# The 71 expert tiles of a Mamba-and-experts block: TensorE's program as straight code, with the weight buffer's half as a register in the address

## What is computed

```python
x = layernorm(x + mamba_layers(x))                      # two layers, states scanned over 512 steps
logits = x @ gate_w + gate_b                            # 8 experts
weights, indices = top_k(logits, 2); weights = softmax(weights)
h = x @ w1[e] + b1[e]                                   # 256 -> 2048, for expert e
xh, gh = split(h, 2)
out_e = (silu(gh) * xh) @ w2[e] + b2[e]                 # 1024 -> 256
x = layernorm(x + sum over the two experts of weight * out_e)
```

## Time and profile before

| | us |
|---|---|
| median of three runs | 1474.63 (1473.24 to 1475.08) |
| the profiled execution | 1472.57 |
| its span, from the first to the last instruction | 1470.7 |
| PE busy with matmuls | 1297.4 (88%) |
| DVE busy | 1087.3 (74%) |
| POOL busy | 807.9 (55%) |
| ACT busy | 791.8 (54%) |

### The profile page before, as it was taken

The page is one execution under the profiler, slowest core; times in us unless marked ns, Lnnn a source line. Parts: engine busy times, 40 slices in busy tenths (PEclk is TensorE's granted clock), DMA queues, the critical chain, the costliest instruction groups (busy, mean ns, idle before and its releaser), DMA issues.

```text
span 1470.7 us, 40051 instructions
## 1 busy us (share of the span) xinstructions
PE 1297.4 (88%) x13108; PEld 1028.9 (70%) x13109; DVE 1087.3 (74%) x2499; ACT 791.8 (54%) x1814; POOL 807.9 (55%) x740
## 2 busy tenths in 40 slices
PE   3889999999999998999872899999999999999970
PEld 1456666656666666666651799999999999999970
DVE  5889999999998898888876566565666565565537
ACT  4656666666666576656540444445444444444434
POOL 2466776766675787677874246060346061052771
PEclk9999999999999998999975899999999999999985
DMA  5203443323343323322512431303030303102594
GB/s 185 98 29 116 130 129 108 97 91 118 103 130 116 108 85 112 115 76 83 180 40 97 148 116 32 118 29 116 31 118 29 121 29 114 36 29 64 136 203 146
DMA packets 94653, 145.70 MB, mean 99 GB/s; under 512 B 13488, under 2 KB 77488, under 8 KB 94448
## 3 DMA queue, kind: packets, MB, share of 16 engines
q1 hardware_dynamic: 79216, 97.06, 20.7%
q0 software_dynamic: 15072, 46.51, 10.6%
q10 hardware_dynamic: 288, 1.19, 0.2%
HBM read 103.06 MB, written 41.67 MB: 98 GB/s over the span
## 4 chain that ended last, share of the span: by engine, by line
PE 60%; DVE 15%; issue 10%; POOL 8%; ACT 3%; SPq 2%; DMA 2%; DVEq 0%; ACTq 0%; POOLq 0%
PE pe L998 13%; PE pa L998 13%; PE py L1010 12%; PE pa L620 4%; PE py L720 3%; POOL arena L2230 3%; DVE arena L1508 3%; PE pa L612 3%; PE pm L756 3%; PE pz L709 2%; PE pt L738 2%; DVE arena L1547 2%; DVE arena L1574 1%; DVE arena L1522 1%; POOL arena L2220 1%
## 5 line engine op out<-in xcount | busy, mean ns | idle before, releaser
L998 PE MATMUL pe<-arena 128*128 128x128 f16 x3408 | 218.5, 220 | 22.5 <-issue 22.5
L998 PEld LDWEIGHTS pe<-arena 128*128 128x128 f16 x3408 | 202.4, 98 | 28.2 <-issue 27.4
L998 PE MATMUL pa<-arena 128*128 128x128 f16 x3408 | 216.1, 219 | 0.0
L1404 ACT ACTIVATE arena<-pe,arena 128x128 f32<-128x128 f32 x568 | 162.2, 372 | 85.1 <-PE pe L998 84.9
L998 PEld LDWEIGHTS pa<-arena 128*128 128x128 f16 x3408 | 198.7, 97 | 0.0
L1010 PE MATMUL py<-arena 128*128 x1704 | 197.6, 273 | 0.8 <-DVE arena L2008 0.8
L1508 DVE SCALAR_TENSOR_TENSOR arena<-pa,arena 128x511 f32<-128x511 f32 (+2 forms) x240 | 178.6, 745 | 7.5 <-ACT arena L1073 1.1
L1980 DVE SCALAR_TENSOR_TENSOR pm<-pa,arena 128x128 f32<-128x128 f32 x284 | 80.6, 352 | 138.1 <-ACT arena L1404 122.6
L1010 PEld LDWEIGHTS py<-arena 128*128 128x128 f16 x1704 | 163.6, 98 | 18.8 <-issue 1.1
L720 PEld LDWEIGHTS py<-arena 128*128 128x128 f32 x1024 | 129.8, 204 | 35.4 <-issue 22.9
L2133 POOL TENSOR_SCALAR arena<-arena 128x1536 f16<-128x1536 f32 (+2 forms) x35 | 42.7, 1220 | 201.8 <-DVE arena L2008 196.8
(11 more groups left out here) (225 smaller groups left out, 2532.5 us busy)
## 6 DMA issues: line engine op xcount, KB each, us to landing
arena<-step_rows SPq DMA_DIRECT2D x64, 512.0 KB, 6.4
arena<-in_w_exp POOLq DMA_DIRECT2D x32, 768.0 KB
arena<-queue SPq DMA_DIRECT2D x74, 129.5 KB, 2.1
answer<-arena SPq DMA_DIRECT2D x71, 128.0 KB, 1.7
arena<-in_x SPq DMA_DIRECT2D x16, 512.0 KB, 6.6
answer<-zeros SPq DMA_DIRECT2D x10, 512.0 KB, 4.7
arena<-h SPq DMA_DIRECT2D x9, 512.0 KB, 6.2
h<-arena SPq DMA_DIRECT2D x8, 512.0 KB, 3.0
```

Source lines behind the costliest of these rows:

```text
L998: ins = pe.matmul(bank[:, f * P:(f + 1) * P], w_split[:, p, hl, d * 2 * FF + col:d * 2 * FF + col + P], x[:, r, d, :], start=(n == 0), sto ...
L1404: ins = e.activation(sg[:, half, f, :], GATE[half][:, f * P:(f + 1) * P], ACT.Silu, bias=b1a[:, bass.ds(ex_, 1), ff], scale=1.0 / S1)
```

## The change

PE's expert stage is written out tile by tile: no loop, no branch on the parity, constant thresholds, no cut through a hidden part. In `hidden` the weights' address is `part(p, ...)` with p as a register, as in `result`. `experts` loads one value per group as before, now ahead of the group's first tile, and the plan no longer holds the two parities. `part` itself, `turn` and `result` stay.

```diff
             def experts(i):
-                v = pe.value_load(plan_i[0:1, bass.ds(i + 2 * NJT, 1)], min_val=0, max_val=2047)
-                return [v % 8, (v // 8) % 8, (v // 64) % 8], (v // 512) % 2, v // 1024
+                v = pe.value_load(plan_i[0:1, bass.ds(i + 2 * NJT, 1)], min_val=0, max_val=511)
+                return [v % 8, (v // 8) % 8, v // 64]
...
-            def hidden(i, r, ex_, halves=(0, 1)):
+            def hidden(i, r, ex_):
                 turn(i, r + 1)
                 pe.wait_ge(w_have, ex_ + 1)
                 pe.sem_inc(hop, 1)
-                by_parity(i, r, ex_ % 2, halves)
-
-            def by_parity(i, r, odd, halves):
-                with pe.If(odd < 1):
-                    products(i, r, 0, halves)
-                with pe.Else():
-                    products(i, r, 1, halves)
-
-            def products(i, r, p, halves):
-                j = WB * i + r
-                for half in halves:
+                j, p = WB * i + r, ex_ % 2
+                for half in range(2):
...
-                                ins = pe.matmul(bank[:, f * P:(f + 1) * P], w_split[:, p, hl, d * 2 * FF + col:d * 2 * FF + col + P],
+                                ins = pe.matmul(bank[:, f * P:(f + 1) * P], part(p, hl, d * 2 * FF + col, P),
                                                 x[:, r, d, :], start=(n == 0), stop=(n == len(passes) - 1))
...
-            ex_, _, _ = experts(0)
-            hidden(0, 0, ex_[0])
-            hidden(0, 1, ex_[1])
-            result(0, 0, ex_[0] % 2)
-            hidden(0, 2, ex_[2], (0,))
-            def whole_group(i):
-                ex_, odd1, odd2 = experts(i)
-                by_parity(i - 1, 2, odd1, (1,))
-                result(i - 1, 1, odd2)
-                hidden(i, 0, ex_[0])
-                result(i - 1, 2, odd1)
-                hidden(i, 1, ex_[1])
-                result(i, 0, ex_[0] % 2)
-                hidden(i, 2, ex_[2], (0,))
-            with pe.Fori(1, NGRP) as i:
-                whole_group(i)
...
+            before = None
+            for i in range(NGRP + 1):
+                ex_ = experts(i)
+                for r in range(WB if i < NGRP else NLEFT):
+                    hidden(i, r, ex_[r])
+                    if before is not None:
+                        result(*before)
+                    before = (i, r, ex_[r] % 2)
+            result(*before)
...
-            dve.tensor_reduce(stj[0:1], cmp_nt[0:1], AX.X, ALU.add)
-            step(dve.tensor_tensor(cmp_[0:1], cmp_[0:1], sign[0:1, :].unsqueeze(1).to_broadcast([1, NJT, NE]), ALU.mult))
-            step(dve.tensor_reduce(ej[0:1], cmp_[0:1, :, 0:NE - 1], AX.X, ALU.add))
+            step(dve.tensor_reduce(stj[0:1], cmp_nt[0:1], AX.X, ALU.add))
...
-            for m in (1, 2):
-                step(dve.scalar_tensor_tensor(packed[:, 1:NG], odd[:, 0:NG - 1, WB - m], float(m * NE ** WB),
-                                              packed[:, 1:NG], ALU.mult, ALU.add))
...
-            pool.iota(sign_i[:, :], [[0, NE // 2], [-2, 2]], base=1, channel_multiplier=0)
...
-            pool.tensor_copy(sign[:, :], sign_i[:, :])
```

More of the change, by code:

```diff
@@ L190, in build @@
         jdum_i = sb("jdum_i", [P, NJT], I32)
-        sign_i = sb("sign_i", [P, NE], I32)
-        sign = sb("sign", [P, NE])
         ARENA = 50400
@@ L286, in build @@
         cmp_, cmp_nt = carve(NJT, NE), carve(NJT, NE)
-        ej, stj, usedj, tmpj = carve(NJT), carve(NJT), carve(NJT), carve(NJT)
+        stj, usedj, tmpj = carve(NJT), carve(NJT), carve(NJT)
         plan_f = carve(3 * NJT + 2 * NE + WB)
@@ L1897, in _ @@
             step(dve.tensor_tensor(cmp_nt[0:1], cmp_[0:1], nt[0:1].unsqueeze(1).to_broadcast([1, NJT, NE]), ALU.mult))
-            dve.tensor_reduce(stj[0:1], cmp_nt[0:1], AX.X, ALU.add)
-            step(dve.tensor_tensor(cmp_[0:1], cmp_[0:1], sign[0:1, :].unsqueeze(1).to_broadcast([1, NJT, NE]), ALU.mult))
-            step(dve.tensor_reduce(ej[0:1], cmp_[0:1, :, 0:NE - 1], AX.X, ALU.add))
+            step(dve.tensor_reduce(stj[0:1], cmp_nt[0:1], AX.X, ALU.add))
             NG = NJT // WB
-            number, odd = e_f.rearrange("p (g r) -> p g r", r=WB), ej[0:1].rearrange("p (g r) -> p g r", r=WB)
+            number = e_f.rearrange("p (g r) -> p g r", r=WB)
             packed = par_f[:, 0:NG]
```

## The result

The changed kernel takes 1667.0 us (median of 4, 1663.48 to 1671.85) against 1474.9 us beside it: a ratio of 1.131 (95% interval 1.129 to 1.133), so 13% slower. The forecast was 1635 us with a range of 1595 to 1700. The profiled execution took 1666.63 us, its span is 1664.9 us.

The account below looks back on a forecast made before the run. The bound was to move from PE to its sequencer: first hidden matmul at 812.2 us, 71 tiles of 10.95 us, 1.4 and 2 us at the end, 35.6 closing, run overhead: 1632.7, rounded up to 1635 us, range 1595 to 1700.

Parts of the forecast that it names:

- the main case: Expert stage bound by PE's sequencer at full clock, 0.127 us an address: 1635 us, held from 1595 to 1665, chance 0.72.
- the case "dearer": Rival: an address costs the 0.140 us of whole tiles, or fetches stall before the end too: 1665 to 1710 us, chance 0.05.
- closing work: Work behind the last result, up to the span's end: 35.6 us, unchanged.
- the step of an address: PE's sequencer needs 0.127 us for each new register address: 8.1 us a tile in the hidden part, 2.0 in the result.
- The waits and the value load: Other sequencer work of a tile: 0.58 us for three waits and the weights' threshold, 0.21 for the group's value load.
- the arithmetic hides: Rival: the sequencer takes only 46 ns an address or works while PE has a queue: 1451 us, chance 0.06.
- The plan: On DVE ahead of the first rows, parity steps go: 1.8 us less, first hidden matmul at 812.2 in place of 813.99.
- The 18 us of gaps are not a second gain: PE's idle gaps at group ends in the loop cost 18 us; under a sequencer bound, removing them saves nothing more.
- the 2 us taken for the end: Allowance for instruction fetches of the straight code, at the end of the expert stage alone: 2 us.
- the rival "clock": PE, empty a third of each hidden part, drops its clock: 1700 us for a fifth of the phase, 1955 for all; chance 0.10.

Follow-up runs that it names:

- e9: The changed kernel with the low-rows pass addressed by a second register, 96 register addresses in a tile's hidden part in place of 64: 1985.8 us, ratio 1.350.
- e1: The changed kernel with the buffer half in the hidden part written in as constants for these inputs, no branch, result part unchanged: 1445.3 us, ratio 0.981.
- e2: The kernel before, loop kept, with only the parity branch of the hidden part replaced by register addresses: 1681.1 us, ratio 1.141.
- e3: The changed kernel, straight code, with the parity branch put back in the hidden part and constant addresses in both arms: 1486.1 us, ratio 1.008.

## Why the prediction came out, point by point

The mechanism was right, and the time lies in the range; the sum to the last result was 36 us short. 1667 us is 2 us above what the main case held (up to 1665): it falls into the strip that the range took in for the case "dearer", which had 0.05.

| step | predicted | measured |
|---|---|---|
| new address instructions | 4544 | 4544 |
| step from one address to the next | 0.127 us | 0.133 mean, 0.124 median |
| a tile | 10.95 us | 11.46 us |
| first hidden matmul | 812.2 us | 815.0 us |
| end of the last result | 1593 us | 1629.3 us |
| closing work | 35.6 us | 35.6 us |
| clock from 830 us on | 1.00 | 1.00 |

**The mis-sized term is the step of an address.** A tile takes 11.46 us from its first hidden matmul to that of the next (mean of the 69 tiles that hold a hidden part and one result). The 63 steps of the hidden part take 8.39 of them (forecast 8.00), the 15 steps of the result 1.97 (1.91), the rest 1.10 (1.04). Together 0.51 us x 71 = 36 us, 32 of them by the steps. The later start adds 2.8 us, and the end takes 2.6 back: 0.8 us beyond the 71 tiles, where 1.4 and 2 were forecast. The median step, 0.124 us, is what rows 6 had given. But the starts of all 4544 show that most often each eighth address takes 150 to 220 ns in place of 124. The prediction took its step from windows of five starts, which mostly miss an eighth; and where a whole tile gave 0.140, it put all of the difference down to the thresholds of lines 1005 and 1007 and a longer first one. Over all 71 result parts the mean step is 0.135 us before and 0.131 after, with constant thresholds: they were worth 0.004 us, the delayed steps 0.007. With the measured mean, 0.133, the prediction's sum gives 1667. The case "dearer" named the size (0.140); the main case's term should have been drawn towards it.

**The waits and the value load** were well sized (1.04 against 1.10 us). That the sequencer needs the 78 ns around each instruction, not only its 46, held; "the arithmetic hides" fell, as e9 shows once more.

**The plan** lost what it was said to lose. Timeline of DVE, the plan's first and last line after the change:

```profile
788.43 0.17 DVE L1850 TENSOR_SCALAR arena<-jrow 128x32 f32<-128x32 f32 x1
...
798.55 0.28 DVE L1888 CAST arena<-arena 1x244 int32<-1x244 f32 x1
```

and before:

```profile
786.30 0.17 DVE L1880 TENSOR_SCALAR arena<-jrow 128x32 f32<-128x32 f32 x1
...
797.95 0.28 DVE L1923 CAST arena<-arena 1x244 int32<-1x244 f32 x1
```

10.1 against 11.65 us, 1.5 us gone (forecast 1.8). But the plan began 2.1 us later in this execution, and the first hidden matmul came 1.0 us later than before, not 1.8 earlier. The step was right about the plan and wrong to expect it in the end time: in the profiled executions of all these kernels, whose Mamba stage is the same code, the first hidden matmul stands anywhere from 808.4 to 820.6 us. This is the 2.8 us by which the stage began later than forecast.

**Branches and fetches.** "The 18 us of gaps are not a second gain" held under the sequencer's bound, and e1 shows that they are one where the sequencer is not the bound: its stage is 28.9 us shorter than before, of which the gaps are 18 by the prediction's count (17.2 in the 21 passes above). The other 11 lie at the end: from the first hidden matmul of the 67th tile on, before takes 59.2 us and e1 48.0. Behind its loop PE stands idle "<-issue" three times, 7.5 us with the 4.0 of rows 10, and e1 never:

```profile
1396.87 1.52 PE L998 MATMUL pe<-arena 128*128 128x128 f16 x24 [1.59 <-issue]
...
1406.79 2.69 PE L998 MATMUL pe<-arena 128*128 128x128 f16 x24 [1.89 <-issue]
```

Fetching straight code cost nothing measurable; the 2 us taken for the end did not show either: all idle time ahead of hidden matmuls is 4.8 us over the whole run (0.9 + 3.9, the page's rows above). Against the rival "clock" stands 1.00 from 830 to 1627 us: PE lacks work in every step, and never for long.

Open: why an address costs 78 ns beyond its instruction, and what the delayed eighth step is.

## What to carry to other kernels

A buffer's half held in a register is not free: it is one sequencer instruction with a step of 0.13 us for each new address on PE, so add up a tile's addresses and waits and compare them with the tile's matmuls; here 48 addresses hid in a tile of 8.2 us and 64 did not, and of the last 16 each cost 7.6 of the 9.4 us that its steps take over 71 tiles. To remove branches from an engine's program, put the choice where few instructions carry it (a branch around many constant addresses, in a loop that stays in place), and read the pace from counts of instructions in a stretch, not from busy shares. When a price is taken from short undisturbed windows, take it over a long stretch as well and explain the difference before choosing the lower.

## What the runs showed of the hardware

- **A delayed step in every eighth address.** The gap between two delayed steps (over 0.145 us) is 8 addresses most often, in the changed kernel (479 of 541 gaps within hidden parts), in e9 (746 of 883) and in e2's loop (423 of 505). In the changed kernel 8 addresses are 32 instructions of PE, in e9 only 24, so it does not go by PE's instructions; in time it is 1.02 to 1.04 us in all three, and whether it goes by addresses or by time these runs don't tell. It is no fetch: e2 fetched 3 packets in 520 us.
- **Straight code is fetched at no cost, until it jumps.** e1: 66 packets and no idle time for them; e3, with a branch a tile: 0.6 us a tile. The loop before is some 1,400 instructions by an estimate from its matmuls (192 for each of three tiles in each of two arms, 64 for each of three results, some 60 others); from 830 to 1380 us it went round some 21 times, and 7 packets were fetched.
- **Starved matmuls look busy.** The page gives PE 1514.9 us after and 1297.4 before, for the same 13108 matmuls: the records last nearly as long as before (225 against 218 ns), and overlap less.
